# A gated cross-attention and feed-forward layer on one core: weights rounded by VectorE, a third batch loaded in blocks, probabilities of three tiles turned through DRAM

## The reference

```python
x = x + tanh(g_xattn) * xattn(layernorm(x), ctx, mask)      # x: 4 x 256 x 256, ctx: 4 x 1601 x 256
x = x + tanh(g_ffn) * ffn(layernorm(x), w_gating, w_linear)

xattn:  scores = h @ ctx.T / sqrt(256); masked to -1e30; attn = softmax(scores); attn @ ctx (0 where all is masked)
ffn:    qdot(a, w) = dot(a.astype(e4m3), w.astype(e4m3)) in bf16
        act = gelu(qdot(h, w_gating[0])) * qdot(h, w_gating[1]);  qdot(act, w_linear)   # 256 -> 1024 -> 256
```

## Time and profile before

| | us |
|---|---|
| time, median of 3 runs | 134.54 |
| runs | 133.6, 134.54, 134.76 |
| time of the profiled execution | 132.98 |
| its span, first to last instruction | 131.2 |
| TensorE busy | 120.9 (92%), 846 matmuls |
| VectorE busy | 89.1 (68%) |
| ScalarE busy | 90.8 (69%) |
| GpSimd busy | 93.2 (71%) |
| DMA | 15.93 MB, queue q1 46.4% of 16 engines' span |

### The profile page before, as it was taken

One profiled execution on the slowest core, in us unless ns is written; L12 is line 12 of the kernel. 1 busy time (PEld: TensorE's weight loads), 2 busy tenths in 40 slices (PEclk: granted clock), 3 DMA queues, 4 the chain that ended last, 5 costly groups with the idle time before them and its releaser, 6 DMA issues.

```text
span 131.2 us, 2509 instructions
## 1 busy us (share of the span) xinstructions
PE 120.9 (92%) x846; PEld 103.1 (79%) x846; DVE 89.1 (68%) x187; ACT 90.8 (69%) x141; POOL 93.2 (71%) x90
## 2 busy tenths in 40 slices
PE   6849999999799999899999899999999959999991
PEld 4438978989789998779999599999987955454780
DVE  1347479989996874998673984394694665767852
ACT  3189999699978893979665680599672876947300
POOL 3069930579999899999999999999989833930000
PEclk9999999999999999999999999999999999999999
DMA  1697999699992997503600069015000000000035
GB/s 44 195 383 229 397 233 261 105 179 188 296 254 102 182 179 126 179 1 85 235 5 0 12 180 308 5 12 148 0 0 7 2 0 0 0 0 5 0 124 196
DMA packets 33908, 15.93 MB, mean 121 GB/s; under 512 B 25700, under 2 KB 32616, under 8 KB 33896
## 3 DMA queue, kind: packets, MB, share of 16 engines
q1 hardware_dynamic: 33608, 15.77, 46.4%
q10 hardware_dynamic: 288, 0.00, 0.1%
HBM read 14.72 MB, written 1.05 MB: 120 GB/s over the span
## 4 chain that ended last, share of the span: by engine, by line
PE 37%; POOL 35%; ACT 8%; DVE 6%; issue 5%; DMA 5%; SPq 1%; POOLq 0%; DVEq 0%; ACTq 0%
POOL ws L436 7%; POOL cTl_a L430 7%; PE scores L774 7%; PE pv L750 6%; POOL wq L437 6%; POOL chl_a L422 5%; PE ring L790 5%; DMA xs<-in_x_dram 5%; PE ring L719 5%; PE pv L754 3%; PE scores L736 3%; PE scores L732 3%; PE scores L737 3%; POOL chl_b L422 2%; POOL cTl_b L430 2%
## 5 line engine op out<-in xcount | busy, mean ns | idle before, releaser
L481 ACT ACTIVATE pT_hi<-ring 128x512 fp32r<-128x512 f32 (+1 forms) x32 | 15.3, 508 | 8.7 <-PE pv L754 4.5
L422 POOL TENSOR_TENSOR chl_a<-cn,chl_a 128x1024 fp32r<-128x1024 f32 x8 | 19.2, 2399 | 1.9 <-ACT chl_a L496 1.9
L599 DVE TENSOR_TENSOR pT_lo<-ring,pT_hi 128x512 fp32r<-128x512 f32 (+1 forms) x32 | 17.8, 578 | 3.3 <-ACT pT_hi L481 3.3
L750 PE MATMUL pv<-chl_a,pT_hi 128*128 128x256 f32 x128 | 18.6, 287 | 0.1
L617 DVE CUSTOM_DVE_ANT_0 sp<-scores,bias 128x1024 f32<-128x1024 f32 (+1 forms) x16 | 15.6, 983 | 4.1 <-PE scores L737 1.9
L422 POOL TENSOR_TENSOR chl_b<-cn,chl_b 128x1024 fp32r<-128x1024 f32 (+1 forms) x8 | 12.5, 1569 | 7.3 <-ACT chl_b L496 6.8
L719 PE MATMUL ring<-ident,sp 128*128 128x128 f32 (+1 forms) x104 | 16.0, 273 | 1.2 <-DVE cTl_b L599 0.7
L750 PEld LDWEIGHTS pv<-chl_a,pT_hi 128*128 128x128 f32 x128 | 16.4, 189 | 0.6 <-DVE xs L636 0.3
L516 ACT ACTIVATE sp<-sp,nb,sc 128x1601 f32<-128x1601 f32 x8 | 13.8, 1724 | 3.5 <-DVE nb L624 3.5
L750 PE MATMUL pv<-chl_b,pT_hi 128*128 128x256 f32 (+1 forms) x80 | 12.8, 291 | 2.2 <-ACT pT_hi L481 1.3
L436 POOL TENSOR_TENSOR ws<-ws,wg 128x1024 f32<-128x1024 f32 x6 | 14.3, 2390 | 0.6 <-DVE wg L641 0.6
(11 more groups left out here) (80 smaller groups left out, 278.0 us busy)
## 6 DMA issues: line engine op xcount, KB each, us to landing
cn<-in_ctx_dram SPq DMA_DIRECT2D x12, 512.0 KB, 4.8
cb<-in_ctx_dram SPq DMA_DIRECT2D x16, 192.0 KB, 3.7
ws<-in_L_ffn_w_gating_dram SPq DMA_DIRECT2D x4, 512.0 KB, 5.4
ws<-in_L_ffn_w_linear_dram SPq DMA_DIRECT2D x2, 512.0 KB, 4.5
out_dram<-xs SPq DMA_DIRECT2D x8, 128.0 KB, 1.8
mrow<-in_mask_BxS_bk_dram SPq DMA_DIRECT2D x4, 200.1 KB, 6.0
xs<-in_x_dram SPq DMA_DIRECT2D x2, 256.0 KB, 5.4
xs<-in_x_dram SPq DMA_DIRECT2D x1, 512.0 KB, 5.1
```

The costliest lines, as they stand in the source:

```text
L422: nc.gpsimd.tensor_tensor(chl(b, g)[0:parts, :, D:2 * D], cn[0:parts, t0:t1, :], chl(b, g)[0:parts, :, 0:D].bitcast(f32), ALU.subtract).th ...
L481: nc.scalar.activation(dst, bank_view(f, size), ACT.Copy, scale=-1.0 if f[0] == "X" else 1.0).then_inc(hi_ready, 1)
L599: nc.vector.tensor_tensor(dst, bank_view(f, size), hi.bitcast(f32), ALU.subtract).then_inc(freed, 1)
L750: nc.tensor.matmul(pv[:, 0:D], pT_hi[0:parts, t, :], ctx[0:parts, t - t0, D * part:D * (part + 1)], start=(t == 0 and part == 0), stop=False)
```

## The change

Three edits, and all five orders are written anew.

1. **Rounding of the weights.** GpSimd's step `I` is gone. VectorE does the maximum and the addition in one instruction and the maximum and the subtraction in a second, so that `wg` stays as ScalarE left it. The result has the opposite sign; the gate activation gets a scale of -1, and the other signs cancel.
2. **Batch 1 in blocks.** `BLOCKED` has batches 1, 2 and 3. Its context is loaded a second time as blocks, and D 1:g takes the place of C 1:0 to C 1:5.
3. **Probabilities of tiles 2, 4 and 6** (`SHUFFLED`). T j:0 to T j:2 go. `R j` on VectorE (not ScalarE's R) turns the 1536 probability columns of the tile in 32x32 blocks into `tb`. SP writes `tb` to a DRAM buffer (`s j`) and reads it back with four DMAs (`t j`) into `pf`, in which each block then lies with the right partitions. `P j:g` on ScalarE copies the high part and on GpSimd subtracts for the low part. T j:3 stays with TensorE.

The query rows are loaded and centred in five parts (tile 0, tile 1, then two tiles each) instead of four; the value buffers are laid out otherwise; `cr` takes the place of the centred rows in `act`, so the first H waits for the last D.

```diff
+    XPART = [(0, 1), (1, 2), (2, 4), (4, 6), (6, 8)]
-    BLOCKED = (2, 3)
+    BLOCKED = (1, 2, 3)
+    SHUFFLED = (2, 4, 6)
+    R4 = P // Q
...
     SP_ORDER = steps("""
-        x0 c0:0 x1 c0:1 c0:3 c0:2 m1 m0 c1:0 x2 c1:1 w0 m2 c1:2 b2 c1:3 c2:0 w1 m3 c2:1 w2 b3 c2:3 w3 c3:1 c2:2
-        c3:3 c3:0 c3:2 w4 w5 o3 o0 o1 o4 o5 o6 o2 o7""")
+        c0:2 x0 c0:1 c0:0 c0:3 x1 m0 x2 b1 c1:3 w0 m1 c1:0 w1 x3 m2 c1:1 b2 c1:2 m3 s2 w2 c2:0 c2:3 t2 b3 w3
+        c2:1 w4 s4 c3:3 c2:2 t4 w5 c3:0 s6 c3:1 c3:2 t6 o1 o0 o3 o2 o5 o4 o6 o7""")
     ACT_ORDER = steps("""
-        K0 R0:0 C0:1 C0:0 X0 R0:1 C0:3 C0:2 R0:2 C0:5 C0:4 C0:6 B0 K1 C1:1 C1:0 X1 E0 W0 T0:0 C1:3 T0:1 R0:3
-        R1:0 C1:2 C1:4 R1:1 T0:2 J E1 T0:3 C1:5 B1 C1:6 D2:0 K2 T1:0 D2:1 W1 T1:2 T1:1 E2 R2:1 X2 T1:3 R2:0 B2
-        T2:0 T2:1 R1:3 R1:2 W2 T2:3 T2:2 D2:2 B3 E3 D3:0 L0 C2:6 T3:1 T3:0 D3:1 K3 T3:3 T3:2 E4 X3 R2:2 R2:3
-        T4:1 T4:0 L1 E5 D3:2 T4:2 T4:3 W3 T5:0 C3:6 T5:2 T5:3 T5:1 R3:0 R3:1 E6 W4 T6:1 L2 L3 N0 T6:0 R3:2 R3:3
-        T6:2 E7 T6:3 N1 T7:0 T7:1 T7:3 L4 W5 H0 T7:2 L5 H1 L6 H2 N2 H3 L7 H4 H5 N3 H6 H7 H8 H9 H10 H11 H12 H13
-        H14 H15""")
+        R0:2 C0:5 C0:4 K0 C0:2 J X0 R0:1 C0:3 R0:3 C0:0 C0:1 C0:6 B0 K1 R0:0 K2 X1 E0 X2 T0:0 T0:1 D1:0 W0 C1:6
+        T0:3 T0:2 D1:1 E1 D1:2 R1:0 B1 T1:0 T1:1 K3 T1:2 W1 E2 R1:1 X3 T1:3 B2 R1:3 D2:0 R1:2 D2:1 L0 K4 D2:2 X4
+        P2:0 T2:3 P2:2 P2:1 C2:6 R2:0 W2 E3 T3:0 T3:1 T3:2 B3 T3:3 E4 D3:0 W3 R2:3 R2:1 D3:1 D3:2 E5 C3:6 R2:2
+        L1 P4:0 P4:1 T4:3 P4:2 E6 T5:1 W4 T5:0 R3:0 L2 N0 T5:3 T5:2 L3 R3:1 R3:2 N1 P6:0 T6:3 P6:1 P6:2 E7 R3:3
+        T7:0 H0 T7:1 W5 T7:2 L4 T7:3 L5 H1 H2 N2 H3 L6 H4 L7 H5 H6 N3 H7 H8 H9 H10 H11 H12 H13 H14 H15""")
     DVE_ORDER = steps("""
-        G0 G1 C0:1 C0:0 X0 C0:3 C0:2 C0:5 C0:4 C0:6 M0:0 M0:1 C1:0 C1:1 X1 G2 M1:0 T0:0 C1:3 M1:1 T0:1 C1:2 G3
-        C1:4 W0 T0:2 D2:0 C1:5 T0:3 O0 C1:6 M2:0 D2:1 M2:1 A0 T1:0 D2:2 T1:1 O1 T1:2 W1 U0 X2 T1:3 O2 M3:0 A1
-        T2:1 T2:0 M3:1 W2 T2:3 T2:2 M4:0 D3:0 D3:1 A2 C2:6 U1 T3:1 T3:0 M4:1 O3 T3:3 T3:2 U2 X3 M5:0 D3:2 M5:1
-        T4:0 T4:1 A3 M6:0 T4:3 T4:2 W3 T5:0 U3 O4 C3:6 A4 T5:3 M6:1 T5:2 T5:1 U4 O5 M7:0 T6:1 O6 T6:0 A5 M7:1
-        T6:2 W4 T6:3 A6 U6 U5 T7:0 T7:3 T7:1 W5 H0 T7:2 O7 H1 A7 U7 H2 H3 H4 H5 H6 H7 H8 H9 H10 H11 H12 Y0 H13
-        H14 Y1 H15 Y2 Y3 Y4 Y5 Y6 Y7""")
+        G0 C0:4 C0:5 C0:2 X0 C0:3 G1 C0:0 C0:1 G2 C0:6 M0:0 M0:1 X1 X2 T0:0 O0 T0:1 D1:0 D1:1 M1:0 C1:6 M1:1
+        D1:2 T0:2 T0:3 W0 G3 M2:0 A0 T1:0 M2:1 T1:1 O1 U0 T1:2 R2 T1:3 D2:0 G4 D2:1 M3:0 X3 A1 O2 D2:2 W1 U1 X4
+        M3:1 T2:3 M4:0 C2:6 W2 A2 T3:0 T3:2 M4:1 T3:1 D3:0 T3:3 R4 D3:1 D3:2 M5:0 O3 M5:1 W3 C3:6 M6:0 A3 M6:1
+        U2 T4:3 U3 O4 R6 T5:1 T5:0 A4 O5 T5:2 M7:0 T5:3 A5 O6 U4 M7:1 U5 T6:3 W4 T7:0 T7:1 H0 O7 A6 T7:2 U6 T7:3
+        W5 H1 H2 A7 U7 H3 H4 H5 H6 H7 H8 H9 H10 H11 H12 H13 H14 Y0 H15 Y1 Y2 Y3 Y4 Y5 Y6 Y7""")
     POOL_ORDER = steps("""
-        F0 Z0:0 Z0:1 F1 Z0:2 Z0:3 Z1:0 Z1:1 v0 I0 F2 D2:0 v1 D2:1 F3 v2 Q0 I1 Z1:3 Z1:2 D2:2 Z2:1 v3 I2 D3:1 Q1
-        D3:0 Z2:0 Z2:3 Z2:2 Q2 D3:2 v4 Q3 I3 v5 Z3:0 v6 Q4 Z3:1 Z3:3 Z3:2 I4 Q5 Q6 v7 Q7 I5""")
+        Z0:2 F0 Z0:3 F1 Z0:1 Z0:0 v0 F2 D1:0 D1:1 D1:2 F3 v1 Z1:0 v2 Q0 Z1:1 Z1:3 D2:0 D2:1 Z1:2 P2:0 P2:1 P2:2
+        D2:2 F4 Z2:0 Q1 v3 D3:0 Z2:3 v4 D3:1 D3:2 Z2:1 P4:0 P4:1 Z2:2 P4:2 Q2 v5 v6 Q3 Z3:0 Z3:1 P6:0 P6:1 Z3:2
+        P6:2 Z3:3 v7 Q4 Q5 Q6 Q7""")
     PE_ORDER = steps("""
-        C0:1 C0:0 X0 C0:3 C0:2 S0:0 C0:5 C0:4 C0:6 S0:1 S0:2 C1:1 S0:3 C1:0 X1 S1:1 S1:0 C1:3 T0:0 T0:1 S1:2
-        S1:3 V0:0 C1:2 C1:4 S2:0 T0:2 C1:5 S2:1 T0:3 V0:1 V0:2 C1:6 T1:0 V0:3 S2:2 S2:3 S3:0 T1:2 S3:1 T1:1 V1:0
-        V1:1 X2 T1:3 S3:3 T2:0 V1:2 T2:3 V1:3 T2:1 S3:2 S4:1 S4:0 T2:2 V2:0 V2:1 V2:2 V2:3 C2:6 S5:1 T3:1 T3:0
-        S5:0 T3:2 S4:3 T3:3 S4:2 X3 V3:0 V3:1 V3:2 S5:2 T4:1 S5:3 V3:3 T4:0 S6:1 T4:2 S6:0 T4:3 V4:0 T5:0 S7:0
-        C3:6 T5:2 V4:1 S6:2 T5:1 V4:2 T5:3 V4:3 S6:3 S7:1 V5:0 V5:1 T6:1 N0 T6:0 S7:3 V5:2 V5:3 T6:3 T6:2 S7:2
-        V6:0 N1 V6:1 V6:2 T7:0 V6:3 H0 T7:3 T7:1 H1 V7:0 T7:2 V7:1 V7:2 V7:3 N2 H2 H3 H4 H5 N3 H6 H7 H8 H9 Y0
-        H10 H11 H12 H13 H14 H15 Y1 Y2 Y3 Y4 Y5 Y6 Y7""")
+        C0:4 C0:5 C0:2 X0 C0:3 S0:2 C0:0 C0:1 C0:6 S0:1 S0:0 S0:3 X1 X2 S1:0 T0:0 T0:1 S1:2 S1:3 T0:2 S1:1 T0:3
+        C1:6 V0:0 V0:1 S2:0 V0:2 T1:1 T1:0 T1:2 S2:1 V0:3 S2:3 S2:2 V1:0 V1:1 X3 T1:3 S3:3 V1:2 V1:3 S3:1 S3:0
+        S3:2 T2:3 X4 C2:6 S4:0 S4:1 V2:0 V2:1 V2:2 V2:3 T3:0 T3:1 T3:2 S4:3 S4:2 T3:3 V3:0 V3:1 V3:2 V3:3 S5:1
+        S5:0 S5:3 S5:2 S6:0 S6:1 C3:6 T4:3 T5:0 S6:2 S6:3 T5:1 S7:1 V4:0 V4:1 S7:0 V4:2 V4:3 N0 T5:3 T5:2 V5:0
+        V5:1 V5:2 T6:3 N1 V5:3 S7:3 S7:2 H0 V6:0 V6:1 T7:0 T7:1 T7:2 H1 V6:2 V6:3 T7:3 H2 V7:0 V7:1 V7:2 V7:3 N2
+        H3 H4 H5 H6 N3 H7 H8 H9 H10 H11 H12 H13 H14 H15 Y0 Y1 Y2 Y3 Y4 Y5 Y6 Y7""")
...
+        tb = sb("tb", [P, R4, NF * Q], f32)
+        scratch = nc.dram_tensor("scratch", [P, R4, NF * Q], f32, kind="Internal")
+        pf = sb("pf", [P, R4, NF * Q], f32)
...
+        def probs(g, hi):
+
+            return (pT_hi if hi else pT_lo)[:, GT * g:GT * (g + 1), :].rearrange("p t (r q) -> p r t q", r=R4)
+
+        def moved(g):
+            return pf[:, :, P * g:P * (g + 1)].rearrange("p r (t q) -> p r t q", q=Q)
+
...
+        def wait_probs(eng, j, g, hi):
+            if g < NG - 1 and j in SHUFFLED:
+                eng.wait_ge(p_hi if hi else p_lo, (act_p if hi else pool_p)[("P", j, g)])
+            else:
+                eng.wait_ge(hi_ready if hi else freed, (act_hi if hi else dve_lo)[("T", j, g)])
...
+            def spill(j):
+                sp_eng.wait_ge(p_turned, dve_r[("R", j)])
+                if spills.index(("s", j)) >= 1:
+                    sp_eng.wait_ge(p_moved, 16 * R4 * spills.index(("s", j)))
+                sp_eng.dma_start(scratch[:, :, :], tb[:, :, :]).then_inc(p_spilled, 16)
+            def move(j):
+                n = moves.index(("t", j))
+                sp_eng.wait_ge(p_spilled, 16 * (spills.index(("s", j)) + 1))
+                if n >= 1:
+                    before = moves[n - 1][1]
+                    sp_eng.wait_ge(p_lo, max(pool_p[("P", before, g)] for g in range(NG - 1)))
+                for c in range(R4):
+                    sp_eng.dma_start(pf[Q * c:Q * (c + 1), :, :],
+                                     scratch[:, c, :].rearrange("(r a) n -> a r n", r=R4)).then_inc(p_moved, 16)
 
...
-            def round_w(i):
-                pool.wait_ge(wg_ready, dve_w[("W", i)])
-                link(nc.gpsimd.tensor_tensor(ws[:, i % 2, :], ws[:, i % 2, :], wg[:, :], ALU.add))
-                nc.gpsimd.tensor_tensor(wq[:, i, :], ws[:, i % 2, :], wg[:, :], ALU.subtract).then_inc(w_ready, 1)
+            def probs_rest(j, g):
+                pool.wait_ge(p_hi, act_p[("P", j, g)])
+                if j >= 1:
+                    pool.wait_ge(weighed, pe_weigh[("V", j - 1, g)])
+                nc.gpsimd.tensor_tensor(probs(g, False), moved(g), probs(g, True).bitcast(f32), ALU.subtract).then_inc(p_lo, 1)
...
+            def probs_hi(j, g):
+                actor.wait_ge(p_moved, 16 * R4 * (moves.index(("t", j)) + 1))
+                if j >= 1:
+                    actor.wait_ge(weighed, pe_weigh[("V", j - 1, g)])
+                nc.scalar.activation(probs(g, True), moved(g), ACT.Copy).then_inc(p_hi, 1)
...
-                                     ACT.Gelu_apprx_tanh).then_inc(gate_ready, 1)
+                                     ACT.Gelu_apprx_tanh, scale=-1.0).then_inc(gate_ready, 1)
...
+            def turn_probs(j):
+                dve.wait_ge(exp_ready, act_e[("E", j)])
+                n = moves.index(("t", j))
+                if n >= 1:
+                    dve.wait_ge(p_spilled, 16 * n)
+                nc.vector.transpose(tb[:, :, :].rearrange("p c (t a) -> p c t a", a=Q),
+                                    sp[:, j % 2, 0:NF * P].rearrange("p (t c a) -> p c t a", c=R4, a=Q)).then_inc(p_turned, 1)
...
+                    if j - 2 in SHUFFLED:
+                        dve.wait_ge(p_turned, dve_r[("R", j - 2)])
...
-            def w_grid(i):
+            def w_round(i):
                 dve.wait_ge(abs_ready, act_w[("W", i)])
-                nc.vector.tensor_scalar(wg[:, :], wg[:, :], GRID_MIN * 2.0 ** 20, None, ALU.max).then_inc(wg_ready, 1)
+                link(nc.vector.scalar_tensor_tensor(out=ws[:, i % 2, :], in0=wg[:, :], scalar=GRID_MIN * 2.0 ** 20,
+                                                    in1=ws[:, i % 2, :], op0=ALU.max, op1=ALU.add))
+                nc.vector.scalar_tensor_tensor(out=wq[:, i, :], in0=wg[:, :], scalar=GRID_MIN * 2.0 ** 20,
+                                               in1=ws[:, i % 2, :], op0=ALU.max, op1=ALU.subtract).then_inc(w_ready, 1)
 
             def hidden(i):
+                if i == 0:
+                    for f in turns:
+                        dve.wait_ge(d_lo, pool_d[f])
                 dve.wait_ge(gate_ready, act_h[("H", i)])
```

(8 more changed lines are left out.)

95 lines of the change are left out of this document (55 added, 40 removed).

## The result

The changed kernel takes 140.79 us (140.46 to 140.97, four runs) beside 134.07 for the kernel before (132.93 to 134.76): ratio 1.056, 95% interval 1.052 to 1.060. It is slower; the prediction was 131.8 with a range up to 138.6. The profiled execution took 140.72, with a span of 138.8 us. Some executions of a kernel run a few per cent longer than the others, mostly at a lower granted clock: ratios and intervals leave them out, medians hold them.

What follows compares the result with a forecast made beforehand. It took TensorE and GpSimd to bound the kernel side by side. Transposes -6.6, lock +2.4 and round trip +1.5 gave -2.7: span 128.5, profiled 130.3, with 1.56 added a median of 131.8 us, range 126.3 to 138.6.

Steps and rivals of the forecast that it cites:

- W1 to W4: Rounding of these four weight tiles on VectorE: waits hidden by TensorE's work ahead (2.8 or 4.6 us), so no more added.
- the sum's whole lock: VectorE's rounding held by GpSimd: one GpSimd subtract waited for lies on the path, +2.4 us in all.
- W0: First weight tile's rounding on VectorE: held ahead of statistics that GpSimd's scales need, +2.4 us on the path.
- GpSimd's side: Sign of the lock's other side: GpSimd subtracts of over 2.6 us beside the rounding passes.
- my 82.5: GpSimd's forecast busy time: 93.2 us less a net 10.7 as rounding goes and new subtracts come.
- Rival (b): Rounding's lock blocks VectorE for 7.2 us a tile, 2.9 on the path; priced at two tiles, 137.6 us; chance 0.24.
- The round trip: Probabilities through DRAM and back: first low half of tile 2 1.5 us later, +1.5; tiles 4 and 6 zero.
- The first term: 60 transposes leave TensorE's full stretch at 0.11 us each, -6.6 us; TensorE's gaps left as they are unless named.
- two engines are bound side by side: The chain of waits before the change: TensorE has 37% and GpSimd 35% of the span.
- The start: Batch 1's blocks land at 20 to 22 us, in time for their subtracts: zero, with +2 as the other end.
- Rival (c): Blocks fill the DMA queue, so tile 2's moved probabilities and a context piece come late: 135.3 us, no change; chance 0.17.
- Rival (a): Rounding passes on VectorE aren't held by GpSimd, so neither lock nor round trip is paid: 126.9 us; chance 0.17.

Runs made afterwards that it cites:

- e8: The e1 kernel without the writes and moves of the probabilities of tiles 2, 4 and 6, whose blocks stay unmoved; 131.81 us.
- e1: The changed kernel with its twelve two-input rounding passes replaced by block turns of the same size with one SBUF input, weights left unrounded; 135.39 us.
- e5: The changed kernel with two steps moved behind tile 4's first two score chunks in TensorE's order, nothing else; 139.89 us, its four runs in two groups.
- h2: The e9 kernel with tile 2's probabilities turned by TensorE again, where the data is ready, and two TensorE steps moved later; 134.57 us.
- g2: The e9 kernel without the writes and moves of the probabilities of tiles 2, 4 and 6, whose blocks stay unmoved; 131.06 us.
- e12: The kernel before with ScalarE writing 8-bit weights, so no rounding on VectorE or GpSimd, orders otherwise kept; 129.98 us, ratio 0.974.
- e9: The changed kernel with ScalarE writing the weights in the 8-bit format and VectorE's twelve rounding passes gone, everything computed; 136.50 us.
- e3: The changed kernel with the rounding edit undone: VectorE takes the maximum, GpSimd adds and subtracts again in the new order; 165.32 us.
- h3: The h2 kernel with the probabilities of tiles 4 and 6 turned by TensorE too, batch 1 still in blocks; 140.54 us.
- e10: The e9 kernel with a second buffer for the context blocks, so batch 2's block loads wait for nothing; 136.15 us.
- e7: The e1 kernel with all twelve probability groups of tiles 2, 4 and 6 turned by TensorE again, without writes and moves; 144.00 us.
- g1: The e9 kernel with batch 1 transposed by TensorE again, only batches 2 and 3 in blocks, the trips kept; 141.00 us.
- e2: The e1 kernel with the passes shrunk to 32 columns, still reading two SBUF inputs, weights unrounded; 136.17 us.

## Why the prediction was wrong

The median of before in the same runs was 134.1. Less 6.6 that gives 127.5. On top of it e8, with neither lock nor trips, still has 4.3 (131.8), the trips add 3.6 (e1) and the lock 5.4: 140.8.

**W1 to W4: "the cover holds, so no more is added".** This step failed, and the sum's whole lock, 2.4, should have been 4.3 to 5.4. W0 was right: GpSimd's scales waited 2.1 us for the statistics, and the exponential of tile 2 begins at 40.95 beside 38.20 in e1, 2.75 later. But W3 alone gave TensorE a wait of 3.0 (in e5's profile the engines met otherwise, and it was 0.25). I had priced only VectorE's side of the lock. GpSimd's side, 9.0 us of busy time (90.7 beside 81.7 in e1; my 82.5 was right without it), was named as a sign and not priced.

**Rival (b)** had this mechanism and a chance of 0.24. It came, on the path twice (W0 and W3), at about the size of my sum's 2.4 plus its 2.9 for one tile. That its price for three tiles, 140.5, is near the result is chance: two other terms filled the place.

**The round trip, +1.5, tiles 4 and 6 zero.** Mis-sized: 3.6 to 5.9. The write was as priced (4.3 for 3.9), the moves took 7.6 where I had taken the low end of 3.9 to 6.1, at a DMA share over 1.1 from 50 to 60. Two things were not in it: C2:6 waiting 1.8 us for a context piece that stood in the queue behind the write, and TensorE at half clock afterwards, S4:0 and S4:1 taking 5.3 us instead of 2.8. Tile 6 was not zero either (V6:0 waited 1.2), nor were tiles 4 and 6 in h2 (2.5).

**The first term, -6.6, "TensorE's gaps I leave as they are".** The matmuls went, but the gaps didn't stay. Without lock and trips TensorE still waits 9.9 us (g2), 3.9 more than before and 6.5 more than in e12:

| | median | TensorE waits | GpSimd busy | GpSimd's share of the chain |
|---|---|---|---|---|
| before | 134.1 | 6.0 | 93.2 | 35% |
| after | 140.8 | 14.9 | 90.7 | 38% |
| e9 | 136.5 | 11.3 | 81.9 | 32% |
| g2 | 131.1 | 9.9 | 81.6 | 27% |
| e12 | 130.0 | 3.4 | 62.8 | none |

I had written that two engines are bound side by side and then made the sum on TensorE alone. Taking the rounding off both engines in the old order (e12: GpSimd 30.4 us less busy, VectorE 7.7) is worth 3.5 us; the new subtracts on GpSimd are in the chain of the changed kernel. That GpSimd's line is what holds g2 is read from its chain (46 to 84 us, nearly unbroken), and ahead of that the same chain runs over the eight loads of batch 2's blocks and their landing, from 29.9 to 43.0. No run took either away alone, e3 gave GpSimd work back in a way that stopped ScalarE, and h3, whose chain has no GpSimd in it, was slow for its own misplaced transposes. So the cause of these last 4.3 us stays open, between GpSimd's line, the blocks and the order.

**The start** was half right: D1:0 waited for no block (it began at 24.95), but TensorE ran at 0.85 of its clock from 11 to 21 and waited 3.0 us for its first two context pieces, where the kernel before waited 1.7 (the third wait of that kind, 1.8, is C2:6's). **Rival (c)** had the queue right in kind: D2:0 began between 42.0 and 45.3 us in every variant with three blocked batches, with one block buffer or two, and in e10, where the loads were asked for 7 us earlier, they took 14.8 us to issue. What that costs isn't known: no run had early blocks and made use of them. **Rival (a)** is out: the passes are held.

## What to carry to other kernels

Before a pass with two SBUF inputs is moved from GpSimd to VectorE, count both sides of the lock, each pass and each GpSimd instruction that meets it, and look at what single small instruction stands behind it on VectorE. Where two engines share the chain of waits, price a saving on both before you add it up. A run that takes work away (e12, from two engines at once) says what that work is worth; one that gives it work back (e3), or puts steps elsewhere (e7, g1), has to be read with its own waits first, for it may measure the new place and not the work. A cast by an engine that already touches the data was better here than moving the arithmetic.

## What was not expected of the hardware

- The lock is mutual and alternates: passes of 1.18 us alone (shortest of L715) took 3.16 and 3.26 us in W3, each ending 1.08 us after the other engine's instruction. The Trainium skill (SBUF — State Buffer, section Who interferes with whom) says that a VectorE instruction with two SBUF inputs contends with a GpSimd one that reads SBUF and that whoever is first blocks the other for all of it; the trace agrees, for both directions, down to passes of 32 columns (e2: up to 2.27 us, 0.18 alone). That section also says that one with at most one SBUF input, outside the two-port modes, doesn't contend; e1's one-input turns, 1.23 to 1.25 us on average, agree.
- ScalarE writes 128x1024 weights as 8-bit numbers in 1.05 us, the same as in f32, and TensorE multiplies them at the same 379 ns per 512 columns (e12).
- After the waits of 1.35 and 1.78 us at 50.5 and 52.9, TensorE's granted clock was 0.66 from 50 to 60; half is the 1.2 GHz level. e1 had 0.67 there. In g2, where one wait of 3.2 us ended at 48.9, it was 0.87, and in e5, where one of 3.3 us ended at 56.2, 0.88.
